# Block attention's pooled queries and output projection on four column groups of TensorE, in a new written order

## The chip, the cores and the metric

The kernel runs on one core of one Trainium2 chip. The metric is the device time of one launch, in microseconds (us). Three runs of the kernel before are shown, and one more execution was taken by the hardware profiler.

## The reference

A decoder of pre-norm layers over x of shape 8 x 256 x 256 (batch row, token, feature), all in fp32. The layers, each added to x, are:

- **a**: attention over features with 16 heads; **b**: a matrix-LSTM cell whose keys and values are the context; **c**: a product-key expert layer (64 gathers of 128 expert rows for each batch row) plus a gated MLP; **d**: causal single-head attention;
- **e**: block cross-attention, the layer that is changed here;
- then six layers of local attention with rotary embedding and a gated MLP.

Layer e, with x already normalised:

```
pooled = x.reshape(B, 16 blocks, 16, D).mean(axis=2)     # 16 pooled tokens of 256
q      = pooled @ Wq                                     # 16 x 1024 (16 heads of 64)
k, v   = ctx @ Wk, ctx @ Wv                              # 256 x 256 each, 4 kv heads
attn   = softmax(where(mask == 0, -1e9, q k^T / 8))
out    = (attn @ v).reshape(16, 1024) @ Wo               # 16 x 256
x     += each of the 16 rows of out, repeated 16 times
```

## The kernel before, in words

The kernel has two blocks, one after the other. `first_layers` computes layers a to e, `local_layers` the six local layers. A new block starts when every engine has ended the old one.

In `first_layers` each of the 8 batch rows passes through about eighty small pieces of work, named by layer (`a_q`, `c_up3`, `e_w0`). The order is written out by hand in `ORDER` (line 58), one list for each queue: tensor, scalar, vector, gpsimd, sync. An entry ("e_w0", -5) says that step s of the loop does this piece for batch row s - 5, so five or six batch rows are under way at once, and `pieces` (line 103) leaves out rows below 0 and above 7. Every engine works strictly through its own list; the lists meet at semaphores. `Slot` (line 240) deals seven PSUM banks out to the pieces of the tensor list in turn: a piece waits for the engine that copied out the piece seven places earlier in its bank.

Layer c sets the traffic between the engines. For each batch row POOL issues 16 groups `c_gather0` to `c_gather15` of four indirect DMAs (line 382) into a ring of four buffers (`RH = 4`). VectorE forms dot products of them (`c_dot`, line 1057), ScalarE a tanh (`c_tanh`) and diagonal matrices (`c_diag`, line 804), and TensorE adds the rows up (`c_up`, line 601), which gives the ring buffer back: `c_gather` j waits for `c_up` j - 4.

The pieces of layer e on TensorE are:

- `e_hT` turns the normalised tile; VectorE sums blocks of 16 tokens into `pooled`, 128 features x 2 halves x 16 blocks (line 1114).
- `e_w0`, `e_w1` (line 671) are the queries: `pooled` is the stationary operand, 128 rows by 16 columns, and 512 columns of `e_wq` stream past for each of two feature halves. Each fills partitions 0 to 15 of one PSUM bank. VectorE copies the first (line 863), ScalarE the second (line 757), into `e_flat`, 16 x 1024.
- `e_q` (line 681) turns that in eight transposes of 16 x 128, and ScalarE copies it to `e_qT`.
- `e_s0`, `e_s1` scores; softmax on VectorE and ScalarE; `e_pT` turns; `e_o` is probabilities times values.
- `e_y` (line 721) is the output projection: eight products, stationary 128 x 16 of `e_o`, moving 128 x 256 of `e_wo`, all added into partitions 0 to 15. ScalarE copies the 16 x 256 result.
- `e_u` (line 729) spreads each of the 16 rows over its 16 tokens with `unpool`, a 16 x 256 matrix of ones and zeros, and VectorE adds it to x.

A fp32 product is two passes through the array, so the trace has two matmuls for each `pe.matmul`; a transpose is one.

POOL makes the constants at the start (`start`, from line 337), and then takes up its list, which begins with `a_rstd` of row 0. SyncE loads the contexts: `b_ctx` (line 277) fills `ctx_b` and `ctx_one` and can begin when `b_cT`, `b_h0` and `b_h1` of the row before are done, and `b_cT`, a turn on TensorE (line 410), waits for it. In the tensor list `b_cT` of row s - 2 stands ten places behind `b_h1` of row s - 3.

Of the kernel before, what the change touches and what calls it, by code (L numbers as in the profile page):

```python
# [20 lines left out]
P = 128  # L21
BATCH, SEQ, D = 8, 256, 256
TILES = SEQ // P
KC = D // P
# [18 lines left out]
def first_layers(nc, xall, x_loaded, ident, ident_bf, shared, dram):  # L43
# [11 lines left out]
    SCALE = 1.0 / 8.0  # L55

# [9 lines left out]
        ("e_s1", -5), ("c_up7", -4), ("c_up8", -4), ("a_k", -1), ("c_up9", -4), ("e_v", -5), ("e_cT", -4), ("e_pT", -5), ("a_q", -1), ("e_o", -5),  # L66
        ("a_z", -1), ("e_y", -5), ("b_hT", -2), ("c_hT", -3), ("e_u", -5), ("c_q0", -3),
    ]
    ORDER["scalar"] = [
# [6 lines left out]
        ("c_diag8", -4), ("c_diag9", -4), ("b_cT", -2), ("e_exp", -5), ("e_v", -5), ("e_cT", -4), ("e_pT", -5), ("a_q", -1), ("e_o", -5),  # L76
        ("c_tanh10", -4), ("c_diag10", -4), ("e_y", -5),
    ]
    ORDER["vector"] = [
# [16 lines left out]
    ]  # L96
    ORDER["sync"] = [
        ("e_ctx", -5), ("e_mask", -4), ("b_ctx", -2),
    ]
    FIRST = max(ahead for order in ORDER.values() for _, ahead in order)  # L100
    LAST = -min(ahead for order in ORDER.values() for _, ahead in order)

# [1979 lines left out]
```

## Time and profile before

| | |
|---|---|
| median of 3 runs | 4052.93 us |
| lowest, highest | 4036.28, 4060.89 us |
| profiled execution | 4046.25 us |
| its span, first to last instruction | 4044.5 us |
| mean granted TensorE clock | 0.972 of full speed |
| first block (layers a to e) | 0 to 1085 us of the span |
| second block (six local layers) | 1085 to 4044.5 us |

Times in a row of the trace are from the start of the span. A line of a timeline gives start, duration, engine, source line, operation, tiles and shapes, the number of instructions merged into it and, in brackets, how long the engine idled before and for what. `128*16 128x256` is a product with a stationary operand of 128 rows by 16 columns and a result of 256 columns. The end of a matmul is modelled and includes the time in the pipeline, so what a piece takes of TensorE is read from the start of its first matmul to the start of the next piece.

### The profile page before, as it was taken

How to read it: one execution, taken by the hardware profiler on the slowest of the kernel's cores; microseconds unless marked ns; L12 is line 12 of the kernel's file. 1: busy time of each engine (PE TensorE's matmuls, PEld its weight loads, DVE VectorE, ACT ScalarE, POOL GpSimd, SP SyncE). 2: the span in 40 equal slices, each digit the busy share in tenths (PEclk: the TensorE clock that was granted, in tenths of full speed). 3: DMA queues.
4: the chain of work that ended last, by engine and by line, in shares of the span. 5: the costliest groups of instructions: out<-in, count | busy, mean ns of one | idle time of the engine just before them, and what ended most of it. 6: DMA issues, size and time to landing. Idle time of an engine off the chain costs nothing.

```text
span 4044.5 us, 75813 instructions
## 1 busy us (share of the span) xinstructions
PE 3814.3 (94%) x25720; PEld 2763.9 (68%) x25720; DVE 2827.7 (70%) x9152; ACT 2275.8 (56%) x6594; POOL 2242.3 (55%) x2091
## 2 busy tenths in 40 slices
PE   7699999897679999999999999999999999999998
PEld 5577777675346777777777777777777777777766
DVE  4577787775367777777777777777777777777763
ACT  2333443343256666666666666666666666666663
POOL 1555565566266555565565565556555556556540
PEclk8899999999789999999999999999999999999999
DMA  3655555567100001000100001000010000010000
GB/s 118 154 155 144 148 154 141 153 164 201 47 1 6 7 8 35 31 12 6 39 16 27 7 6 37 17 29 4 7 39 14 29 7 27 16 31 14 5 7 27
DMA packets 110543, 210.95 MB, mean 52 GB/s; under 512 B 22321, under 2 KB 71505, under 8 KB 108625
## 3 DMA queue, kind: packets, MB, share of 16 engines
q0 software_dynamic: 40960, 134.25, 12.7%
q1 hardware_dynamic: 69056, 71.71, 5.5%
q8 instruction: 210, 3.44, 0.4%
q14 instruction: 173, 1.41, 0.1%
q10 hardware_dynamic: 144, 0.13, 0.0%
HBM read 191.39 MB, written 2.10 MB: 48 GB/s over the span
## 4 chain that ended last, share of the span: by engine, by line
PE 67%; issue 2%; DVE 2%; POOL 1%; ACT 1%; DMA 0%; SPq 0%; DVEq 0%; POOLq 0%; ACTq 0%
PE pj L1594 23%; PE pj L1674 12%; PE y_ps L1657 8%; PE y_ps L1683 6%; PE sc L1622 5%; PE o_ps L1648 4%; PE tp L1633 4%; PE tp L1602 4%; PE tp L1572 1%; POOL l_qk_rot L1535 1%; ACT l_probs L1753 0%; DVE l_probs L1890 0%; POOL l_r_q L1540 0%; DVE l_qk_cos L1866 0%; POOL l_r_k L1540 0%
## 5 line engine op out<-in xcount | busy, mean ns | idle before, releaser
L1594 PE MATMUL pj<-w_qkv,l_xT 128*128 128x512 f32 x2304 | 1063.1, 598 | 7.2 <-DMA l_qk_gain<-in_gains 3.6
L1535 POOL TENSOR_TENSOR l_qk_rot<-l_qk_cos,l_qk_sin 128x512 f32<-128x512 f32 x384 | 564.8, 1471 | 840.5 <-DVE l_qk_sin L1869 555.7
L382 POOL DMA_INDIRECT f_rows<-in_emb,f_expert x512 | 514.6, 1005 | 382.2 <-PE facc L601 175.0
L1594 PEld LDWEIGHTS pj<-w_qkv,l_xT 128*128 128x128 f32 x2304 | 413.5, 191 | 385.8 <-issue 375.9
L1753 ACT ACTIVATE l_probs<-l_probs,l_low 128x128 f32<-128x128 f32 x1536 | 594.0, 391 | 2.4 <-DVE l_low L1890 0.6
L1674 PE MATMUL pj<-l_xnT,l_w 128*128 128x256 f32 x2112 | 510.9, 387 | 2.2 <-issue 1.2
L1861 DVE TENSOR_REDUCE l_ss<-l_qk_sq 128x8 f32<-128x512 f32 x384 | 261.6, 681 | 324.9 <-ACT l_qk_sq L1740 173.3
L1890 DVE CUSTOM_DVE_ANT_0 l_probs<-sc,l_shut,l_r_q 128x128 f32<-128x128 f32 x1536 | 440.2, 344 | 54.4 <-PE tp L1633 46.7
L1718 ACT ACTIVATE l_qk_raw<-pj 128x512 f32<-128x512 f32 x384 | 227.0, 591 | 434.6 <-PE pj L1594 419.6
L1674 PEld LDWEIGHTS pj<-l_xnT,l_w 128*128 128x128 f32 x2112 | 383.9, 190 | 65.0 <-issue 17.4
L1657 PE MATMUL y_ps<-w_o,l_oT 128*128 128x256 f32 x1536 | 341.2, 380 | 3.5 <-ACT l_oT L1718 3.5
L1657 PEld LDWEIGHTS y_ps<-w_o,l_oT 128*128 128x128 f32 x1536 | 292.8, 191 | 63.9 <-issue 22.0
L1540 POOL TENSOR_TENSOR l_r_q<-l_ssm,l_minus_half 128x8 f32<-128x8 f32 x192 | 320.4, 1669 | 16.0
L1540 POOL TENSOR_TENSOR l_r_k<-l_ssm,l_minus_half 128x8 f32<-128x8 f32 x192 | 320.4, 1669 | 16.0
L1866 DVE TENSOR_TENSOR l_qk_cos<-l_qk_raw,l_rope 128x512 f32<-128x512 f32 x384 | 302.2, 787 | 0.0
L601 PE MATMUL facc<-f_rows,f_diag 128*128 128x256 f32 x1024 | 266.5, 410 | 32.8 <-ACT f_diag L804 25.5
L1921 DVE TENSOR_SCALAR l_hT<-pj,l_ff_cols 128x256 f32<-128x256 f32 (+1 forms) x282 | 135.2, 480 | 231.6 <-ACT l_gate L1781 231.6
L1753 ACT ACTIVATION_READ_ACCUMULATOR l_probs<-l_probs,l_low 128x1 f32 x1536 | 291.8, 190 | 0.0
L1683 PE MATMUL y_ps<-l_w,l_hT 128*128 128x256 f32 x1128 | 266.3, 386 | 0.6 <-DVE l_hT L1928 0.6
L1633 PEld LDWEIGHTS tp<-identity,l_probs 128*128 128x128 f32 x1536 | 180.7, 141 | 119.4 <-issue 97.0
L601 PEld LDWEIGHTS facc<-f_rows,f_diag 128*128 128x128 f32 x1024 | 205.7, 207 | 78.7 <-issue 39.6
L1633 PE MATMUL tp<-identity,l_probs 128*128 128x128 f32 x1536 | 239.8, 279 | 14.6 <-DVE l_probs L1900 5.7
(324 smaller groups left out, 7164.6 us busy)
## 6 DMA issues: line engine op xcount, KB each, us to landing
w_qkv<-in_L_ffn_Wqkv SPq DMA_DIRECT2D x12, 1024.0 KB
l_w<-in_ff_w SPq DMA_DIRECT2D x6, 1408.0 KB, 6.1
f_rows<-in_emb,f_expert POOLq DMA_INDIRECT x512
w_o<-in_L_ffn_Wo SPq DMA_DIRECT2D x6, 1024.0 KB
w_qkv<-in_L_ffn_Wqkv SPq DMA_DIRECT2D x12, 512.0 KB
l_xf<-l_stream SPq DMA_DIRECT2D x48, 128.0 KB
l_xf<-l_stream SPq DMA_DIRECT2D x48, 127.0 KB
l_w<-in_ff_w SPq DMA_DIRECT2D x6, 768.0 KB, 4.9
```

The source lines that it names most:

```text
L382: pool.indirect_dma_start(rows[:, j % RH, k, :], None, dram["emb"], bass.IndirectOffsetOnAxis(ap=expert[:, n % 2, at:at + 1], axis=0)).the ...
L601: last = pe.matmul(acc[:, j // (HALVES // TILES), :], diag[:, j % 2, k, :], rows[:, j % RH, k, D:2 * D], start=(first and k == 0), stop=(f ...
L1535: pool.tensor_tensor(qk_rot[:, i % ROTS, :], qk_cos[:, b, :], qk_sin[:, b, :], ALU.add).then_inc(rotated if s == 0 else pool_front, 1)
L1540: pool.tensor_tensor(inv_norm, ssm[:, b, :], minus_half[:, :], ALU.pow).then_inc(pool_front, 1)
L1594: last = pe.matmul(pj[b][:, :], xT[:, k, t * P:(t + 1) * P], w_qkv[:, k, s * INNER + c * 512:s * INNER + (c + 1) * 512], start=(k == 0), s ...
L1633: last = pe.transpose(bank[:, at:at + P], probs[:, u % 2, 2 * p + x, t * P:(t + 1) * P], ident[:, :])
L1657: last = pe.matmul(y_ps[:, t, :], oT[:, k, t * P:(t + 1) * P], w_o[:, k, :], start=(t == 0 and k == 0), stop=(t == TILES - 1 and k == HP - 1))
L1674: last = pe.matmul(pj[b][:, s * SEQ:(s + 1) * SEQ], w_1[:, k, at:at + P], xnT[:, k, :], start=(k == 0), stop=(k == KC - 1))
L1683: last = pe.matmul(y_ps[:, t, :], hT[:, f, t * P:(t + 1) * P], w_2[:, f, :], start=(f == 0), stop=(f == FC - 1))
L1753: last = nc.scalar.activation(tile, tile, ACT.Exp, bias=low[:, u % 2, at, t:t + 1], scale=-1.0, accum_out=p_sum[:, u % 2, at, t:t + 1])
L1866: nc.vector.tensor_tensor(cos, raw, table(0, 0, DH), ALU.mult)
L1890: last = nc.vector.tensor_tensor_reduce(probs[:, u % 2, at, t * P:(t + 1) * P], sc[x][:, cols], shut[:, t, :], r_q[:, par, t, h:h + 1], 3. ...
```

## The change

It does four things.

1. `e_w0` and `e_w1` become one piece `e_w`. The 1024 query columns are taken as four groups of 256. Group g writes PSUM partitions 32g to 32g + 31, so each group uses its own 32 columns of the array. The stationary operand is 32 columns of `pooled`, 16 of them real and 16 that belong to the next half or to a new block of zeros. One copy (ScalarE, 128 x 256) takes the place of two, and `e_q` is two transposes of 128 x 128 in place of eight small ones, copied out by ScalarE with a strided view.
2. `e_y` is done the same way: four column groups each sum two of the eight products. The four partial sums stay on four sets of partitions, ScalarE copies 128 x 256, and `e_u` adds them, because `unpool` now has four copies of its pattern on 128 partitions, with zero rows between.
3. POOL makes two more zero fills and three copies of `unpool` (32 x 256 each) before its last constant semaphore.
4. All five lists of `ORDER` are new. `b_cT` moves to the start of the next step, behind `c_s2`; `b_ctx` comes first in SyncE's list; `f_rstd` stands before `c_gather14`; `c_y1` and many of the `c_m` and `c_up` pieces change places.

```diff
-        ("c_up5", -4), ("b_h0", -3), ("e_w0", -5), ("b_h1", -3), ("e_w1", -5), ("c_up6", -4), ("e_q", -5), ("a_hT", -1), ("b_cT", -2), ("e_s0", -5),
-        ("e_s1", -5), ("c_up7", -4), ("c_up8", -4), ("a_k", -1), ("c_up9", -4), ("e_v", -5), ("e_cT", -4), ("e_pT", -5), ("a_q", -1), ("e_o", -5),
-        ("a_z", -1), ("e_y", -5), ("b_hT", -2), ("c_hT", -3), ("e_u", -5), ("c_q0", -3),
+        ("c_q1", -4), ("c_q0", -4), ("e_cT", -5), ("b_hT", -3), ("c_s0", -4), ("c_s1", -4), ("c_up10", -5), ("c_s3", -4), ("c_s2", -4), ("b_cT", -3),
+        ("c_up11", -5), ("a_v", -2), ("c_m0", -4), ("c_m1", -4), ("c_m2", -4), ("c_m3", -4), ("c_m4", -4), ("c_up12", -5), ("b_g", -3), ("c_m5", -4),
...
+        ("b_qk2", -3), ("b_qk3", -3), ("e_hT", -5), ("c_up5", -4), ("b_h0", -3), ("b_h1", -3), ("a_hT", -1), ("e_w", -5), ("c_up6", -4), ("e_q", -5),
+        ("a_k", -1), ("e_s1", -5), ("e_s0", -5), ("c_up7", -4), ("a_q", -1), ("c_up8", -4), ("e_v", -5), ("c_y1", -4), ("e_pT", -5), ("c_up9", -4),
+        ("e_o", -5), ("a_z", -1), ("e_y", -5), ("c_hT", -3), ("e_u", -5),
...
-        ("c_gather13", -4), ("c_gather14", -4), ("a_rstd", 0), ("c_gather15", -4), ("f_rstd", -5), ("c_gather0", -3), ("c_gather1", -3),
+        ("f_rstd", -5), ("c_gather14", -4),
...
-        ("e_ctx", -5), ("e_mask", -4), ("b_ctx", -2),
+        ("b_ctx", -3), ("e_ctx", -4), ("e_mask", -4),
...
-        pooled = sb("pooled", [P, KC, NB])
+        pooled = sb("pooled", [P, KC + 1, NB])
...
+                pool.wait_ge(set_step, made[0])
+                for g in range(1, 4):
+                    pool.tensor_copy(unpool[g * QUAD:(g + 1) * QUAD, :], unpool[0:QUAD, :]).then_inc(set_step, 1)
...
-                    for k in range(KC):
-                        last = pe.matmul(s.bank[0:NB, :], pooled[:, k, :], e_wq[:, k, i * 512:(i + 1) * 512], start=(k == 0), stop=(k == KC - 1))
+                both = pooled[:, :, :].rearrange("p k n -> p (k n)")
+                for k in range(KC):
+                    for g in range(4):
+                        last = pe.matmul(s.bank[g * QUAD:(g + 1) * QUAD, 0:SEQ], both[:, k * NB:k * NB + QUAD], e_wq[:, k, g * 256:(g + 1) * 256],
+                                         start=(k == 0), stop=(k == KC - 1), skip_group_check=True)
...
-                for c in range(8):
-                    last = pe.transpose(s.bank[:, c * NB:(c + 1) * NB], e_flat[:, c * P:(c + 1) * P], ident[0:NB, 0:NB])
+                for c in range(2):
+                    last = pe.transpose(s.bank[:, c * P:(c + 1) * P], e_w[:, c * P:(c + 1) * P], ident[:, :])
...
-                for c in range(8):
-                    last = pe.matmul(s.bank[0:NB, 0:D], e_o[:, c * NB:(c + 1) * NB], e_wo[:, c, :], start=(c == 0), stop=(c == 7))
+                for h in range(2):
+                    for g in range(4):
+                        c = 2 * g + h
+                        last = pe.matmul(s.bank[g * QUAD:(g + 1) * QUAD, 0:D], e_o[:, c * NB:c * NB + QUAD], e_wo[:, c, :], start=(h == 0), stop=(h == 1), skip_group_check=True)
```

## Rows read from the trace of the kernel before

**Rows 1.** The page's head and its busy time of each engine.

```profile
span 4044.5 us, 75813 instructions
PE 3814.3 (94%) x25720; PEld 2763.9 (68%) x25720; DVE 2827.7 (70%) x9152; ACT 2275.8 (56%) x6594; POOL 2242.3 (55%) x2091
```

**Rows 2.** Busy time by stretch: bounds, length, PE, PEld, DVE, ACT, POOL, clock, DMA.

```profile
278.00:945.00 667.00, 614.53 (x3070) 475.64 (x3068) 507.29 (x2085) 258.78 (x787) 402.02 (x403) 0.96 0.58 152
945.00:1057.00 112.00, 72.80 (x298) 52.39 (x298) 43.52 (x184) 30.29 (x100) 49.94 (x50) 0.85 0.53 152
```

**Rows 3.** The block sums of line 1114, one for each batch row.

```profile
L1114 DVE TENSOR_REDUCE f_pooled<-fp x8: 691/691/692, 277.9 to 1056.7; 128x32 f32<-128x512 f32 x8
```

**Rows 4.** Waits of PE from 278 to 945 us: total, times, longest.

```profile
PE fp L410 <- DMA f_ctx_one<-in_ctx: 10.6, 5, 2.7
PE facc L601 <- ACT f_diag L804: 6.3, 4, 3.1
```

**Rows 5.** Timeline of PE around `e_w0`, `e_w1` and `e_q` of one batch row.

```profile
512.50 1.89 PE L601 MATMUL facc<-f_rows,f_diag 128*128 128x256 f32 x8
514.22 1.00 PE L535 MATMUL fp<-f_ctx_one,f_b_c 128*128 128x65 f32 x8
515.16 1.89 PE L671 MATMUL fp<-f_e_wq,f_pooled 128*16 128x512 f32 x4
516.98 0.44 PE L544 MATMUL fp<-f_ctx_one,f_b_c 128*128 128x65 f32 x2
...
518.91 1.89 PE L671 MATMUL fp<-f_e_wq,f_pooled 128*16 128x512 f32 x4
520.73 1.99 PE L601 MATMUL facc<-f_rows,f_diag 128*128 128x256 f32 x8
522.65 0.67 PE L681 MATMUL fp<-identity,f_e_p 16*128 16x16 f32 x8
523.25 0.66 PE L410 MATMUL fp<-identity,f_h_ad 128*128 128x128 f32 x4
```

**Rows 6.** Timeline of PE around `e_y` of the same batch row.

```profile
541.51 3.63 PE L721 MATMUL fp<-f_e_wo,f_e_o 128*16 128x256 f32 x16
545.07 0.66 PE L410 MATMUL fp<-identity,f_h_be 128*128 128x128 f32 x4
```

**Rows 7.** Timeline of PE in the second block: scores, then probabilities times values.

```profile
2006.49 1.10 PE L1622 MATMUL sc<-l_kT,l_qT 64*64 64x128 f32 x32
2007.53 3.72 PE L1674 MATMUL pj<-l_xnT,l_w 128*128 128x256 f32 x16
...
2012.92 0.44 PE L1648 MATMUL o_ps<-l_pT,l_v 128*64 128x128 f32 x4
2013.19 0.28 PE L1648 MATMUL o_ps<-l_pT,l_v_mid 128*64 128x64 f32 x4
...
2013.97 0.70 PE L1594 MATMUL pj<-w_qkv,l_xT 128*128 128x512 f32 x1
```

**Rows 8.** Timeline of PE at the end of the first block, batch row 7.

```profile
1057.50 5.13 PE L671 MATMUL fp<-f_e_wq,f_pooled 128*16 128x512 f32 x8 [0.83 <-issue]
1063.36 0.64 PE L681 MATMUL fp<-identity,f_e_p 16*128 16x16 f32 x8 [0.72 <-issue]
...
1077.05 5.62 PE L721 MATMUL fp<-f_e_wo,f_e_o 128*16 128x256 f32 x16 [0.37 <-ACT f_e_o L757]
1083.13 1.13 PE L729 MATMUL fp<-f_e_y,f_unpool 16*128 16x256 f32 x4 [0.46 <-ACT f_e_y L757]
```

**Rows 9.** POOL's gathers by line from 278 to 945 us: busy, mean ns, idle before.

```profile
L382 POOL DMA_INDIRECT f_rows<-in_emb,f_expert x367 | 369.4, 1007 | 262.1 <-PE facc L601 129.9 <-issue 104.1 <-remote 26.3
```

**Rows 10.** Timeline of POOL: a gather late in the first block.

```profile
1009.13 0.95 POOL L382 DMA_INDIRECT f_rows<-in_emb,f_expert  x1 [5.89 <-PE facc L601]
```

**Rows 11.** Timeline of POOL at the start of the span.

```profile
1.60 0.29 POOL L2002 CAST identity_bf<-identity 128x128 bf16<-128x128 f32 x1
...
9.55 0.72 POOL L369 TENSOR_TENSOR f_rstd_a<-f_var_eps_a,f_minus_half 128x2 f32<-128x2 f32 x1 [0.18 <-POOL f_g_raw L337]
```

**Rows 12.** VectorE's copy of `e_w0`: ns least, median, most.

```profile
L863 DVE COPY f_e_p<-fp x8: 678/679/679, 283.8 to 1061.0; 16x512 f32<-16x512 f32 x8
```

More of the change, by code:

```diff
@@ L662, in e_v_, with e_w_ @@
                 by_token("e_v", n, ctxT_e, e_wv)
-            def e_w(i):
-                def queries(n):
-                    pe.wait_ge(loaded["e"], 16 * LOADS["e"])
-                    pe.wait_ge(e_pooled, n + 1)
-                    s = Slot(f"e_w{i}", n)
-                    wait(pe, s.taken, s.before)
-                    for k in range(KC):
-                        last = pe.matmul(s.bank[0:NB, :], pooled[:, k, :], e_wq[:, k, i * 512:(i + 1) * 512], start=(k == 0), stop=(k == KC - 1))
-                    last.then_inc(ps_full, 1)
-                return queries
+            def e_w_(n):
+                pe.wait_ge(loaded["e"], 16 * LOADS["e"])
+                if n == 0:
+                    pe.wait_ge(consts_set, 2)
+                pe.wait_ge(e_pooled, n + 1)
+                s = Slot("e_w", n)
+                wait(pe, s.taken, s.before)
+                both = pooled[:, :, :].rearrange("p k n -> p (k n)")
[3 more added lines that the diff above has]
+                                         start=(k == 0), stop=(k == KC - 1), skip_group_check=True)
+                last.then_inc(ps_full, 1)
             def e_q(n):
-                copied("e_w0", n)
-                copied("e_w1", n)
+                copied("e_w", n)
                 s = Slot("e_q", n)
                 wait(pe, s.taken, s.before)
-                for c in range(8):
-                    last = pe.transpose(s.bank[:, c * NB:(c + 1) * NB], e_flat[:, c * P:(c + 1) * P], ident[0:NB, 0:NB])
+                for c in range(2):
+                    last = pe.transpose(s.bank[:, c * P:(c + 1) * P], e_w[:, c * P:(c + 1) * P], ident[:, :])
                 last.then_inc(ps_full, 1)
@@ L739, in _ @@
                        "b_h0": b_h0, "b_h1": b_h1, "c_q0": c_q(0), "c_q1": c_q(1), "c_y0": c_y(0), "c_y1": c_y(1),
-                       "d_q": d_q, "d_k": d_k, "d_v": d_v, "d_s": d_s, "d_pT": d_pT_, "d_o": d_o, "e_cT": e_cT, "e_k": e_k, "e_v": e_v_, "e_w0": e_w(0), "e_w1": e_w(1), "e_q": e_q,
+                       "d_q": d_q, "d_k": d_k, "d_v": d_v, "d_s": d_s, "d_pT": d_pT_, "d_o": d_o, "e_cT": e_cT, "e_k": e_k, "e_v": e_v_, "e_w": e_w_, "e_q": e_q,
                        "e_s0": e_s(0), "e_s1": e_s(1), "e_pT": e_pT_, "e_o": e_o_, "e_y": e_y_, "e_u": e_u})
@@ L830, in e_exp, with e_q @@
                 last.then_inc(e_exped, 1)
+            def e_q(n):
+                s = Slot("e_q", n)
+                act.wait_ge(ps_full, s.full)
+                wait(act, ps_full, last_before("e_q", n, "e_s0 e_s1"))
+                F(e_qT[:, :, :].rearrange("p a n -> p (a n)").rearrange("p (g c q) -> p g c q", g=4, c=2),
+                  s.bank[:, 0:2 * P].rearrange("p (c g q) -> p g c q", c=2, g=4)[:, :, :, 0:NB], ACT.Copy).then_inc(s.taken, 1)
             do = {f"b_m{h}": b_m(h) for h in range(H4)}
@@ L845, in _ @@
                 "e_cT": copy_of("e_cT", flat(ctxT_e[:, :, :]), "e_k e_v"), "e_k": copy_of("e_k", flat(e_kT[:, :, :]), "e_s0 e_s1"),
[L846 to L848 removed]
+                "e_v": copy_of("e_v", flat(e_v[:, :, :]), "e_o"), "e_w": copy_of("e_w", e_w, "e_pT", SEQ), "e_q": e_q, "e_exp": e_exp,
+                "e_pT": copy_of("e_pT", e_pT[:, :, :, :].rearrange("p t g n -> p (t g n)"), "d_o e_o"), "e_o": copy_of("e_o", e_o[:, 0:8 * NB], "e_y", 8 * NB),
+                "e_y": copy_of("e_y", e_y[:, :], "e_u", D)})
             for piece, n in pieces("scalar"):
@@ L1112, in e_hT @@
                 dve.wait_ge(ps_full, s.full)
-                wait(dve, ps_full, last_before("e_hT", n, "e_w0 e_w1"))
-                V.tensor_reduce(flat(pooled[:, :, :]), s.bank[:, :].rearrange("p (kb j) -> p kb j", j=BLK), AX, ALU.add).then_inc(e_pooled, 1)
+                wait(dve, ps_full, last_before("e_hT", n, "e_w"))
+                V.tensor_reduce(flat(pooled[:, 0:KC, :]), s.bank[:, :].rearrange("p (kb j) -> p kb j", j=BLK), AX, ALU.add).then_inc(e_pooled, 1)
                 dve.wait_ge(e_pooled, n + 1)
@@ L1178, in _ @@
                        "d_k": copy_of("d_k", flat(k_ad[:, :, :]), "a_z d_s"), "d_top": d_top_, "d_inv": d_inv_, "d_o": d_o,
[L1179 removed]
+                       "e_hT": e_hT, "e_mask": e_mask, "e_s": e_s, "e_low": e_low, "e_probs": e_probs, "e_u": add_tiles("e_u")})
             gained = False
```

38 lines of the change are left out of this document (18 added, 20 removed), and 37 rows, old and new, of the table ORDER.

## The prediction

> **What bounds the kernel now.** I read the page first, then busy time by stretch, then the waits of TensorE, and last its timeline around the changed pieces. The page alone shows PE busy for 94% of the span [rows 1], but that is a mean over two blocks, and the change touches only the first, which ends at 1085 us. The second block runs the same instructions afterwards, so I take its 2959 us as fixed.
>
> Inside the first block the block sums of layer e mark the beat: eight of them from 277.9 to 1056.7 us [rows 3], so (1056.7 - 277.9) / 7 = 111.3 us for a batch row. From 278 to 945 us, six such periods, PE is busy 614.5 of 667 us, VectorE 507, ScalarE 259, POOL 402 [rows 2]. POOL has a hidden part: between its gathers it idles for "issue" for 104 us in all [rows 9], which it cannot avoid, so it is occupied for 506 us. In order of occupation: PE 92%, VectorE 76%, POOL 76%. PE's own waits are small and scattered. The largest, 10.6 us in five waits, is the turn `b_cT` waiting for its context; the next is 6.3 us [rows 4]. A batch row therefore costs about 102.4 us of PE (614.5 / 6) and 8.8 us of idle. In these six periods a microsecond taken from PE is worth close to a microsecond. From 945 to 1057 us PE is busy only 72.8 of 112 us [rows 2]: the last row's gathers go round the ring with little beside them, and latency sets the time.
>
> **The price of a pass.** Eight passes of 256 columns take 514.22 - 512.50 = 1.72 us, 0.215 us each [rows 5]. So 128 columns cost about 0.108 us.
>
> **`e_w`.** Before, two pieces take 516.98 - 515.16 and 520.73 - 518.91, 1.82 us each, 3.64 us together [rows 5]. Afterwards it is 2 halves x 4 groups x 2 passes = 16 passes of 256 columns, the same number of streamed columns. All depends on whether the four groups stream side by side, which no row shows for four groups of 32 columns. The bounds: not at all side by side, 16 x 0.215 = 3.44 us, no gain; all four, 4 x 0.215 = 0.86 us. The nearest rows are two. The scores run in 64*64 tiles, two row halves and two column halves: 32 passes of 128 columns begin at 2006.49 and the next piece at 2007.53, 1.04 us against 32 x 0.108 = 3.46 us in series, 3.3 times faster [rows 7]. Probabilities times values use two column groups over all 128 rows: 8 passes of 128 and 16 of 64 columns would be 1.72 us in series and take 2013.97 - 2012.92 = 1.05 us, 1.6 times faster; their first four passes take 0.27 us where perfect pairs would need 0.22 [rows 7]. So different tiles overlap, four at once too, and products of two passes each do not prevent it. I take four at once, because the scores have four tiles in the same order of issue, and add 0.10 us for the irregular first pass: 0.96 us. The gain is 2.7 us.
>
> **`e_y`.** Before 545.07 - 541.51 = 3.56 us [rows 6]. After, 16 passes in four rounds as above, 0.96 us; gain 2.6 us.
>
> The Trainium skill ("TensorE: Matmul & The Clock Gate", the section on packing small matmuls) gives a speedup of 2.38 for three column groups and 3.07 for four row groups. With 3.07 in place of 3.6 each piece would take 1.12 us and the gain over eight rows would be about 2.6 us less; the 3.3 of rows 7 lies between. The skill's "TensorEngine Tiling", key properties, says that changing the tiling mode drains the engine, which speaks against two short tiled pieces between full-array ones; rows 5 to 7 show such a change at a tenth of a microsecond, and that is in my 0.96.
>
> **`e_q`.** Eight small transposes take 523.25 - 522.65 = 0.60 us [rows 5]. Two of 128 columns at 0.108 plus 0.10 are 0.32 us; gain 0.3 us. Bounds: 0.2 and 0.4.
>
> **`e_u`** keeps four passes of 256 columns; its contraction grows from 16 to 128 partitions. That could only matter if rows cost time; the 64-row and 128-row products of rows 7 are priced by columns. I take 0, bounds 0 and 0.2 us.
>
> **Sum for TensorE**: 2.7 + 2.6 + 0.3 = 5.6 us for a batch row.
>
> **Six full periods**: 6 x 5.6 = 33.6 us. The gaps that remain must not grow for this to hold.
>
> **The period 945 to 1057**: here a shorter `e_w` and `e_y` of row 6 help only where the ring waits for them. It does: POOL idled 5.89 us for a `c_up` that stands behind `e_y` and `e_u` [rows 10]. Bounds 0 and 5.6 us; I take 4.
>
> **The tail, row 7**: nothing stands beside layer e here, and the clock is often at its lower level. From the start of `e_w0` to `e_q` are 1063.36 - 1057.50 = 5.86 us; eight passes took 5.13 us, so four rounds of half the columns at that pace take 1.3 us, at the lower level 4 x 0.43 = 1.7 us, plus 0.4 us of pipeline and 0.5 us for one copy: 2.6 us, gain 3.2. `e_y` goes from 5.62 us [rows 8] to 1.0 to 1.9 us, gain 3.8. Together 7 us; bounds 5 and 8.
>
> **Order: `b_cT`.** It stands ten places behind `b_h1` of the row before, whose buffers its load needs, and waited 10.6 us in five rows [rows 4]. In the new order it stands in the next step, and the load is first in SyncE's list, so the transfer has more than 30 us of TensorE pieces over it. The waits vanish. But `b_hT` and `b_cT` leave the end of the step, where they covered `e_y`'s copy; `c_hT` (0.44 us) covers that now. What is late next is `c_up` behind `c_diag` (6.3 us, [rows 4]). I count half, 5 us; bounds 0 and 11.
>
> **Order, the rest**: `c_m0` to `c_m4` now stand in one run behind `a_v`, six pieces of 1.72 us, so `c_up11` and `c_up12` are 10.3 us apart, and `c_gather0` of the next row waits for `c_up12`. POOL has 27 us of waiting in a period ((129.9 + 26.3) / 6, [rows 9]) and must give up 5.6 of it. `f_rstd` before `c_gather14` costs nothing: it waits for the statistics behind `e_u`, and `c_gather14` waits for `c_up10`, which stands later than `e_u` on TensorE. I take 0; bounds a gain of 20 and a loss of 80 us (below).
>
> **Constants**: three copies of 32 x 256 and two fills on POOL stand before `a_rstd` of row 0, which starts right behind the constants at 9.55 us and on which the first turn waits. A cast of 128 x 128 took 0.29 us [rows 11]; three at 0.3 to 0.4, two fills and one more wait give 1.5 us of delay. Bounds 0.5 and 2.5.
>
> **Copies**: VectorE loses one of 0.68 us a row [rows 12], ScalarE's two become narrower in columns. Both engines are below 80%; what hides them is PE. I count 0.
>
> **Sum**: 33.6 + 4 + 7 + 5 - 1.5 = 48 us less than the profiled 4046.25 us, 3998 us. The median of the runs, 4052.9, lies 6.7 us above the profiled execution; from there it would be 4005. I forecast 4002 us.
>
> **Rivals.**
>
> *The period does not follow PE.* PE loses 5.6 us but the ring or VectorE's place in the order gives half back, or idler stretches bring more of the lower clock. The clock is 0.96 from 278 to 945 us [rows 2], so 8% of the time is at the lower level, costing at most 27 us; half as much again would take 13 us. For it: POOL's waits and the falls of the clock behind idle stretches. Against it: no engine but PE is above 80%. Saving 15 to 38 us, 4026 us.
>
> *Groups go two at a time.* Two full-height column groups are all that rows 7 show. Then `e_w` and `e_y` take 1.82 us each, 1.7 us a row more than forecast: 14 us, so 4016 us. *In series*: nothing is left but `e_q`, one copy and the order: 48 - 8 x 5.0 = 8 us, 4042 us; rows 7 speak against it.
>
> *The new order closes more gaps.* PE idles 8.8 us a period; were another 3 us of it gone, 6 x 3 = 18 us and some in the first 278 us: 3978 us.
>
> *Slower: the ring.* POOL's floor is 506 / 6 = 84 us a period, its waits 27. The run of `c_m` pieces between `c_up11` and `c_up12` makes `c_gather0` and all fifteen behind it late; TensorE then waits for `c_diag`. It decides once the waits pass 27 us a period. At 33 us, a period is 117 us: 7 x 6 = 42, less the tail's 7 and plus 1.5, 4083 us. Against it: before, `c_up10` and `c_up11` were nearly as far apart, about 9 us (three `c_m`, `e_k` and four `c_s`), and the ring bore it.
>
> **Chances.** Forecast 0.50 (3988 to 4014); more gaps closed 0.10; period follows by half 0.19; two at a time 0.07; in series 0.05; slower 0.09. A change below 1% (40 us) can't be told from none. Faster by over 1%: 0.8 of the forecast's 0.50, the 0.10, and 0.04 of the rest, 0.54. Slower by over 1%: 0.07. Within: 0.39. The range is 3976 to 4038: it leaves out the series case, the slower one and the end of the best one.
>
> **What would show it.** In the changed trace: `e_w` as 16 matmuls of `128*32 128x256` from whose first start to the next piece are about 1 us (2: two at a time; 3.5: series); the same for `e_y`; block sums 105 us apart; no wait of a turn for `f_ctx_one`; POOL's waits for line 601's successor below 20 us a period; the second block 2959 us long. I am wrong if the block sums stay 111 us apart while `e_w` takes 1 us: then PE was not what set the period.

## The result, and the profile after

The changed kernel took 4093.7 us, median of four runs (4082.0 to 4105.2), beside 4053.9 us of the kernel before in the same comparison: ratio 1.0104, 95% interval 1.0084 to 1.0125. It is 1% slower; the forecast was 4002 us. The profiled execution lasted 4082.0 us, its span 4080.3 us. The experiments below ran on several chips, and these split in two kinds: on three of them, the slow kind, the kernel before takes 4047 to 4055 us and the changed kernel loses about 1%; on two, the fast kind, the kernel before takes 3994 to 3995 us and the changed kernel gains 1.3%. The first comparison behaves as the slow kind. One slow chip was used in two comparisons and was slow in both; each of the others was used once, so that the kind belongs to the chip, and not to the hour, is likely and not shown. Most of what follows is the search for what the kinds differ in.

The page's head and the windows of the first comparison. Columns of the windows: stretch, its length, busy time of PE, PE's loads, VectorE, ScalarE, POOL, then granted clock, share of the DMA engines, GB/s.

```profile
span 4080.3 us, 75857 instructions
...
PE 3809.2 (93%) x25736; PEld 2777.8 (68%) x25736; DVE 2816.2 (69%) x9144; ACT 2272.3 (56%) x6594; POOL 2249.0 (55%) x2096
...
273.30:1015.80 742.50, 630.18 (x3156) 501.73 (x3155) 509.70 (x2132) 261.96 (x813) 426.24 (x423) 0.90 0.56 144
...
1097.00:1120.00 23.00, 15.07 (x78) 8.59 (x78) 6.51 (x9) 4.47 (x14) 0.00 (x0) 0.57 0.00 1
1120.00:4080.00 2960.00, 2897.47 (x21312) 2057.80 (x21312) 2107.41 (x6220) 1900.59 (x5465) 1673.26 (x1500) 0.99 0.06 18
```

The second block takes 2960 us, as before. The whole loss is in the first block, which ends at 1120 us in place of 1085. The rows are not of one length: the first six, from the first block sum to the seventh, take 695.0 us before and 742.5 us now, and the last one 83.8 and 81.0. So the comparison that counts is over those six rows, the first window above against the same one of the kernel before:

```profile
277.90:972.90 695.00, 632.61 (x3149) 490.50 (x3148) 518.26 (x2139) 266.26 (x813) 420.59 (x422) 0.96 0.58 153
```

The idle time of PE grew from 62 to 112 us. Its busy time is the same although each row gives it less to do, because the granted clock is 0.90 in place of 0.96: it falls behind the idle stretches, and the same matmuls then take longer. Idling and the lower clock together ate the saving. The marks of the beat, and the tiled matmuls (ns least, median, most; first and last start):

```profile
L682 PE MATMUL fp<-f_e_wq,f_pooled x128: 379/379/634, 277.3 to 1098.9; 128*32 128x256 f32 x128
L1133 DVE TENSOR_REDUCE f_pooled<-fp x8: 691/692/692, 273.3 to 1096.8; 128x32 f32<-128x512 f32 x8
```

The block sums are (1096.8 - 273.3) / 7 = 117.6 us apart, where [rows 3] had 111.3; this mean of seven is the "period" of the tables below. Now the waits of PE from 273 to 979 us (sum, times, longest), to be held against [rows 4]:

```profile
PE fp L691 <- ACT f_e_p L769: 18.9, 6, 3.8
PE fp L741 <- ACT f_e_y L769: 14.1, 2, 7.0
PE facc L598 <- DVE x_all L1108: 13.4, 2, 6.8
PE fp L741 <- issue: 10.9, 4, 6.3
```

`b_cT`'s wait for its context is gone, as forecast. In its place PE waits for ScalarE's copies of `e_w` and `e_y`, although a copy takes 0.38 us. The timelines of PE and of ScalarE over one batch row say why:

```profile
641.91 0.61 PE L418 MATMUL fp<-identity,f_h_ad 128*128 128x128 f32 x4
642.45 1.07 PE L682 MATMUL fp<-f_e_wq,f_pooled 128*32 128x256 f32 x16
643.45 1.30 PE L609 MATMUL facc<-f_rows,f_diag 128*128 128x256 f32 x4
...
648.96 0.44 PE L691 MATMUL fp<-identity,f_e_p 128*128 128x128 f32 x2 [1.75 <-ACT f_e_p L769]
```

```profile
641.37 1.26 ACT L816 ACTIVATE f_diag<-identity,f_coef 128x128 f32<-128x128 f32 x4
648.03 0.60 ACT L769 ACTIVATE f_hT_ad<-fp 128x512 f32<-128x512 f32 x1 [5.40 <-remote]
648.52 0.38 ACT L769 ACTIVATE f_e_p<-fp 128x256 f32<-128x256 f32 x1
```

The turn `a_hT` (the instructions of L418) ends at 642.5, `e_w` (L682) at 643.5 (1.0 us for 16 matmuls, as forecast), and the copies of both start at 648.0 and 648.5. ScalarE stood idle for 5.4 us, and VectorE, waiting for `b_h1`, as well. The releaser is given as "remote", which is what the view prints when a signal came and no instruction that gives it ended then. Elsewhere a waiting engine starts 0.04 to 0.07 us behind the end of the matmul. The ends of matmuls are modelled, but PE works in order and had long started the next piece. So by the trace the data were there, and the signal was not.

### The profile page after: what moved, and what is told of

Read it like the earlier page. It is cut to its first block, busy times and chain, and to the rows that moved or that the text cites. A ratio compares the mean times of both kernels' runs of the same rounds, so it can differ in the third digit from the quotient of the medians.

```text
span 4080.3 us, 75857 instructions
## 1 busy us (share of the span) xinstructions
PE 3809.2 (93%) x25736; PEld 2777.8 (68%) x25736; DVE 2816.2 (69%) x9144; ACT 2272.3 (56%) x6594; POOL 2249.0 (55%) x2096
## 4 chain that ended last, share of the span: by engine, by line
PE 66%; issue 2%; DVE 2%; POOL 1%; ACT 1%; DMA 0%; SPq 0%; DVEq 0%; POOLq 0%; ACTq 0%
PE pj L1613 23%; PE pj L1693 12%; PE y_ps L1676 8%; PE y_ps L1702 6%; PE sc L1641 5%; PE tp L1652 4%; PE o_ps L1667 4%; PE tp L1621 4%; PE tp L1591 1%; POOL l_qk_rot L1554 1%; ACT l_probs L1772 0%; DVE l_probs L1909 0%; DVE l_qk_cos L1885 0%; POOL l_r_q L1559 0%; DMA l_xf<-l_stream 0%
## 5 line engine op out<-in xcount | busy, mean ns | idle before, releaser
L609 PE MATMUL facc<-f_rows,f_diag 128*128 128x256 f32 x1024 | 279.4, 420 | 30.8 <-issue 15.5
```

The lines of the kernel that those rows point to most:

```text
L609: last = pe.matmul(acc[:, j // (HALVES // TILES), :], diag[:, j % 2, k, :], rows[:, j % RH, k, D:2 * D], start=(first and k == 0), stop=(f ...
```

## The experiments

In all tables "period" is the distance of the block sums, mean of seven. A signal is the increment of a semaphore, by which one engine tells another that it is done. "Silences" are pauses of over 2.5 us between two recorded signals of the compute engines (the DMA's signals left out) from 250 to 1130 us; they are counted from the signals' times in the trace, which the views don't print. Some belong to every kernel: on the fast kind there are 6 to 12 (22 to 41 us), most of them at the thinly filled end of the first block. On the slow kind a part of the signals is not recorded, so a pause can also be a lost record. A second measure is safer: "remote" is the sum of ScalarE's and VectorE's waits that have this releaser, as in the line at 648.03 us above, from 260 to 1130 us. A lost record can hide such a wait and can't make one. It is 0 in every kernel on the fast kind.

The expectations name theories by letters: T, the tiled pieces cost the time; O, the new order costs it; M, the late signals do; K, the kernel itself is slow at times; D, crowds of short matmuls bring the silences; P, TensorE's own work brings them; G, POOL's gathers bring them.

### First comparisons, which fell on the fast kind

`tiled_old_order`: the tiled pieces in the order of before (the list entries `e_w0`, `e_w1` become one `e_w`).

```diff
-("c_up5", -4), ("b_h0", -3), ("e_w0", -5), ("b_h1", -3), ("e_w1", -5), ("c_up6", -4), ("e_q", -5)
+("c_up5", -4), ("b_h0", -3), ("b_h1", -3), ("e_w", -5), ("c_up6", -4), ("e_q", -5)
```

> The tiled e_w, e_q, e_y and e_u in the order of the kernel before (e_w stands where e_w1 stood, e_w0's place is left out). Theory T, the tiled pieces themselves cost the time (they look 1 us long, but their copies start 5 to 7 us after their modelled end): block sums at least 116 us apart, first block about 1115 us, whole kernel 4080 to 4100 us. Theory O, the new order costs it: TensorE gets 5.6 us less a row and the period follows at least by half, block sums 105 to 109 us apart, 4005 to 4035 us.

`untiled_new_order`: the code of before with the new lists, `("e_w0", -5), ("e_w1", -5)` standing for `("e_w", -5)`.

> The new order with the pieces of the kernel before: e_w0 and e_w1 stand together where e_w stands, e_y is eight passes over 16 rows. Theory O (order): as slow as the changed kernel or slower, since TensorE has 5.6 us more to do a row, 4090 to 4140 us, block sums 117 to 123 us apart. Theory T (tiled pieces): the order is worth what its removed wait of b_cT is, so 4040 to 4060 us, block sums 110 to 112 us apart, and copies start at once when TensorE's pieces end.

`e_y_untiled` and `e_w_untiled`: the changed kernel with one of the two pieces put back.

```diff
-                for h in range(2):
-                    for g in range(4):
-                        ...
+                for c in range(8):
+                    last = pe.matmul(s.bank[0:NB, 0:D], e_o[:, c * NB:(c + 1) * NB], e_wo[:, c, :], start=(c == 0), stop=(c == 7))
```

> The changed kernel with e_y alone put back to eight passes into 16 rows (e_u takes 16 rows again). Theory T: half of the tiled pieces' cost goes, e_y's copy starts at the piece's end, 4065 to 4085 us. Theory O: e_y is 2.6 us longer in each row, so 4095 to 4115 us.

> The changed kernel with e_w alone put back to e_w0, e_w1 and the eight small transposes, e_y on four groups. Theory T, each four-group piece costs by itself: it lies between the new order without tiling (ratio 0.994) and with e_w tiled (0.990), or above both if e_y is the harmful one (0.995 to 1.005). Theory O, the order alone decides and a piece on four groups saves what its modelled time says, 2.6 us a row: 0.987 to 0.991.

`two_groups`: `QUAD = 64`, two column groups, `e_w[g * QUAD:(g + 1) * QUAD]` over 512 columns each, four transposes in `e_q`.

> The changed kernel with two column groups of 64 in place of four of 32: e_w is 8 passes of 512 columns in pairs, e_y 8 passes of 256 in pairs, e_q four transposes, partial sums in two groups. By the modelled times each piece takes 1.8 us in place of 1.0. Theory O: 1.6 us more a row, 4095 to 4115 us. Theory T, if the delay hangs on tiles of 32 columns: the delay goes, 4040 to 4065 us; if on tiling of any kind: 4090 to 4110 us and the same late copies.

The kernel before stood at 3995 us, so the changed kernel itself and the kernel before were run again:

> The changed kernel once more, since the four kernels run so far stood beside a kernel before of 3995 us, not 4053. If it loses 1% again (ratio 1.008 to 1.013), the copies that start 5 to 7 us after the modelled end of their pieces belong to the kernel and will be in this trace too. If the loss belongs to the chip of the first comparison, the late copies are gone (under 0.1 us) and the ratio is 0.985 to 0.995, as two groups and the e_y of before gave 0.987 and 0.990.

> The kernel before, for its trace under the same conditions as the others. Block sums 108 to 112 us apart; if PE's completion signals come in bunches only in the first comparison, every copy behind an idle ScalarE starts 0.04 us after its piece here.

| fast kind | us | ratio (95%) | period | silences |
|---|---|---|---|---|
| before_again | 3990.5 (before: 3993.9, 7 runs) | | 105.4 | 8, 31 us |
| tiled_old_order | 3992.6 | 0.9990 (0.9978 to 1.0002) | 106.5 | 12, 41 us |
| untiled_new_order | 3966.0 | 0.9938 (0.9918 to 0.9957) | 102.8 | 10, 36 us |
| e_y_untiled | 3954.1 | 0.9898 (0.9877 to 0.9918) | 101.0 | 6, 23 us |
| e_w_untiled | 3952.0 | 0.9897 (0.9880 to 0.9913) | 101.1 | 7, 26 us |
| two_groups | 3941.5 | 0.9869 (0.9852 to 0.9886) | 99.3 | 8, 27 us |
| changed_again | 3941.4 | 0.9869 (0.9853 to 0.9886) | 98.9 | 7, 22 us |

Theories T and O both fall on this kind: nothing costs time here, and the first four expectations all put the time too high. `before_again` has a period of 105.4 us where 108 to 112 were expected (its first six rows are 108.8 us each, the last one 85). The same program as in the first comparison gains 52 us. Its `e_y`, first PE, then ScalarE:

```profile
490.40 1.07 PE L733 MATMUL fp<-f_e_wo,f_e_o 128*32 128x256 f32 x16
491.40 0.65 PE L418 MATMUL fp<-identity,f_hc 128*128 128x128 f32 x4
491.98 1.13 PE L741 MATMUL fp<-f_e_y,f_unpool 128*128 128x256 f32 x4
```

```profile
491.54 0.38 ACT L769 ACTIVATE f_e_y<-fp 128x256 f32<-128x256 f32 x1 [0.68 <-PE fp L733]
```

The copy starts 0.07 us behind the piece, in each of eight rows. With the old order the tiles gain 0.1%, within the noise, and the waits of PE in `tiled_old_order` (267 to 920 us; the same two lines come out for 264 to 924) show where the gain went:

```profile
PE fp L418 <- DMA f_ctx_one<-in_ctx: 22.2, 5, 5.3
PE fp L418 <- DVE f_hc L914: 15.6, 6, 5.3
```

`before_again` waits 9.3 and 5.5 us there. Over the first six rows of each, PE's busy time fell from 618.6 to 593.6 us, 4.2 us a row, and `b_cT` and `c_hT` (the turns of L418 above), whose data come when they come, took 23 of the 25 us. For `b_cT` the list shows why: it is the fifth piece behind `b_h1`, not the tenth as the text ahead of the prediction has it, so four pieces cover the load of its context, and the tiles shorten two of them. The new order is what lets the tiles' gain through on this kind.

### Is it the chip, and what do late copies cost?

`changed_third` is the changed kernel again. `late_changed` and `late_before` hold back copies by hand (in `late_before` the piece `e_w1` stands for `a_hT`):

```diff
+                    for _ in range({"a_hT": 9, "e_y": 14}.get(name, 0)):
+                        chain.link(F(dst, s.bank[0:parts, 0:width], ACT.Copy))
                     F(dst, s.bank[0:parts, 0:width], ACT.Copy).then_inc(s.taken, 1)
...
+                    for _ in range(27 if t == 1 else 0):
+                        chain.link(V.tensor_copy(late[:, :], s.bank[:, 0:P]))
```

> The changed kernel once more, because two comparisons of it disagree: ratio 1.0104 with the kernel before at 4054 us, 0.987 with it at 3994 us. Theory M (the loss came with the silences of the engines' signals, which the first pair of traces shows and the later ones do not): if the kernel before takes about 3990 us here, the ratio is 0.985 to 0.989 and block sums are 101 to 105 us apart; if it takes 4040 us or more, the ratio is above 1.0 and silences of 3 to 7 us are back in the trace. Theory K (the kernel itself is sometimes slow): a ratio above 1.0 beside a kernel before of 3990 us.

> The changed kernel with three copies made late by hand in every row: VectorE does 27 small copies of a bank ahead of its work on b_h1, ScalarE repeats a_hT's copy nine times and e_y's fourteen times ahead of the one that signals, about 5.4 us each, at the places where the first trace of the changed kernel shows copies 5 to 7 us late. Theory M: the delays at b_h1 and a_hT lie beside each other, so the row is longer by most of 2 x 5.4 us, block sums 110 to 115 us apart in place of 102.3, 4000 to 4035 us. If ScalarE and VectorE have room for them (they are busy 40% and 75%), the row is longer by less than 4 us, 3940 to 3970 us, and theory M needs another path from the late signals to the period.

> The same delays in the kernel before: 27 small copies of VectorE ahead of its work on b_h1, nine more copies of e_w1, fourteen more of e_y, about 5.4 us each. If the order before bears late copies better than the new one (b_hT, b_cT and c_hT stand behind e_y, a wider cover), it loses 2 to 6 us a row, 4010 to 4040 us, and the changed kernel's gain is smaller or gone under delays. If both bear them alike, it loses what the changed kernel loses, 4050 to 4090 us, and the loss of the first comparison is due to where the silences fell, not to the order.

This chip was of the slow kind. `changed_third` took 4086.6 us beside 4048.3, ratio 1.0092 (1.0076 to 1.0109), with 47 silences, 194 us; the traces of the first comparison have 52 (204 us) for the changed kernel and 37 (131 us) for the one before, and on the fast kind the first five rows of these two kernels have none. This is theory M: the loss goes with the late signals. PE, ScalarE and POOL of `changed_third` around `e_y`:

```profile
560.77 1.07 PE L733 MATMUL fp<-f_e_wo,f_e_o 128*32 128x256 f32 x16
561.78 0.66 PE L418 MATMUL fp<-identity,f_hc 128*128 128x128 f32 x4
569.54 2.07 PE L741 MATMUL fp<-f_e_y,f_unpool 128*128 128x256 f32 x4 [7.11 <-ACT f_e_y L769]
```

```profile
560.57 1.26 ACT L816 ACTIVATE f_diag<-identity,f_coef 128x128 f32<-128x128 f32 x4
569.11 0.38 ACT L769 ACTIVATE f_e_y<-fp 128x256 f32<-128x256 f32 x1 [7.27 <-remote]
```

```profile
561.48 0.95 POOL L390 DMA_INDIRECT f_rows<-in_emb,f_expert  x1 [0.30 <-issue]
562.73 0.95 POOL L390 DMA_INDIRECT f_rows<-in_emb,f_expert  x1 [0.30 <-issue]
563.98 0.95 POOL L390 DMA_INDIRECT f_rows<-in_emb,f_expert  x1 [0.30 <-issue]
565.24 0.95 POOL L390 DMA_INDIRECT f_rows<-in_emb,f_expert  x1 [0.30 <-issue]
566.49 0.95 POOL L390 DMA_INDIRECT f_rows<-in_emb,f_expert  x1 [0.30 <-issue]
```

From row to row `e_y`'s copy starts 0.6, 6.4, 7.3, 6.6, 2.4, 2.3, 7.2 and 0.1 us behind its piece; in `changed_again` it is 0.07 us in all eight. The silence lies over a run of gathers 1.25 us apart. Two of its places come back in nearly every row (1 to 4 us and 32 to 37 us behind the block sum), in the first comparison and on this chip, but two thirds of the silences lie elsewhere. The delays by hand cost both kernels alike: `late_changed` took 4207.3 us (+121 against `changed_third`), `late_before` 4165.9 (+118 against 4048.3). I had expected 4000 to 4035 us and 4010 to 4040 or 4050 to 4090 us, with the fast kind in mind, and delays of 5.4 us each; what they tell is the difference, some 15 us a row. The delays were larger than meant on VectorE (18 of its copies take 5.8 us, so 27 take 8.7) and 5.6 and about 5.4 us on ScalarE. Late copies are dearly paid in either order, and the new order is not more tender; it meets more of them: ScalarE and VectorE wait 185 us for late signals in the changed kernel's first trace and 51 us in that of the kernel before.

### What brings the silences?

Theory D was that they follow crowds of short matmuls, of which the tiled pieces (16 in 1 us) make more.

```diff
-("c_up5", -4), ("b_h0", -3), ("b_h1", -3), ("a_hT", -1), ("e_w", -5), ("c_up6", -4), ("e_q", -5), ("a_k", -1)
+("b_h0", -3), ("c_up5", -4), ("b_h1", -3), ("a_hT", -1), ("c_up6", -4), ("e_w", -5), ("a_k", -1), ("e_q", -5)
```

That is `spread_changed`; `split_before` cuts the matmuls of before in quarters and halves. Its quarters share a bank, and of their partial sums only a part is kept, so it is read for its time alone:

```diff
+                        for q in range(4):
+                            last = pe.matmul(s.bank[0:NB, q * P:(q + 1) * P], pooled[:, k, :], e_wq[:, k, i * 512 + q * P:i * 512 + (q + 1) * P], ...
```

> The changed kernel with TensorE's list alone edited, so that long passes stand between the short ones: b_h0, c_up5, b_h1, a_hT, c_up6, e_w, a_k, e_q in place of c_up5, b_h0, b_h1, a_hT, e_w, c_up6, e_q, a_k, and a_z, e_pT, c_up9, e_o, c_y1, e_y in place of c_y1, e_pT, c_up9, e_o, a_z, e_y. Theory D: with the kernel before at 4050 us, the silences at +4 and +32 us shrink and the kernel is 20 to 80 us faster than the changed one, ratio 0.990 to 1.004; with the kernel before at 3990 us the edit does nothing, 0.985 to 0.990. If density is not the cause, it keeps the changed kernel's ratio on either chip, 1.009 or 0.987, within 0.003.

> The kernel before with the same columns in shorter matmuls: each matmul of e_w0 and e_w1 in four of 128 columns (16 a piece in place of 4), each of e_y in two of 128. By columns TensorE's time is unchanged. Theory D: with the kernel before at 4050 us it is slower by 15 to 80 us, ratio 1.004 to 1.02, with silences behind these pieces; with the kernel before at 3990 us there is no difference, 0.998 to 1.004. If density is not the cause, no difference on either.

> Two column groups of 64 again. Theory D (on some chips, those where the kernel before takes 4040 to 4060 us, dense runs of short matmuls bring silences of the signals; e_w and e_y on four groups are 16 matmuls in 1 us each, on two groups 8 in 1.8 us): with the kernel before at 4050 us here, ratio 0.990 to 1.003, so better than the changed kernel's 1.009, and the silences at +4 and +32 us of each row are shorter than 3 us. If only the chip and the order decide: ratio 1.007 to 1.015 there, same silences. With the kernel before at 3990 us: 0.987 again.

> The new order with the pieces of the kernel before again. With the kernel before at 4050 us here: theory D says the dense tiled pieces are gone, ratio 0.990 to 1.003, few silences; if the order itself is what meets the silences, ratio 1.010 to 1.020, as TensorE has 5.6 us more a row. With the kernel before at 3990 us: 0.994 again.

Theory D falls on every count: `split_before` is 1.0010, `spread_changed` at 1.0143 is slower than the changed kernel where the theory wanted it faster (and outside the 0.003 that "density is not the cause" allowed), and `untiled_new_2`, with no tiled piece in it, loses as much as the changed kernel. It is the order that loses on this kind, by 35 us, where it gains 29 on the other. The silences don't sort these kernels: `spread_changed` has 149 us of them and is the slowest, `split_before` has 155 and loses nothing. The waits for late signals do: 127 to 191 us in the four kernels with the new order, all of which lose, and 50 to 60 us in those with the old order, which don't. They still don't rank the four among themselves. Streaks of gathers, less than 1.7 us from start to start, were what was left. In the six rows behind the first block sum 39 of the 40 silences of `changed_third` begin inside a streak of four or more gathers, and such streaks cover 61% of that time. Streaks of eight or more are 12 to 16 in the old order (226 us in `before_again`) and 26 in the new one on the fast kind (412 us in `changed_again`); on the slow kind they are 16 (173 us) in the kernel before and about 30 (some 320 us) in `changed_third`. The new order keeps POOL's gathers running, which is what one wants of it. Two kernels test that: one leaves out three of four gathers, the other breaks the streaks and keeps all gathers.

```diff
-                    for k in range(HALF):
+                    for k in range(HALF if n == 0 else 1):
```

```diff
                         pool.indirect_dma_start(rows[:, j % RH, k, :], None, dram["emb"], ...)
+                    for _ in range(4):
+                        pool_chain.link(pool.tensor_copy(late[:, :], ident[:, :]))
```

> The changed kernel with fewer gathers: of the four gathers of each piece only the first is issued in the rows after the first one (the other slots keep old rows, so layer c adds something else); everything else is as it was. Theory G (on the slow kind of chip the signals fall silent where gathers follow each other without a pause; every silence seen stands in or behind such a streak): with the kernel before at 4050 us, no silences of over 2.5 us in rows 1 to 4, block sums 97 to 103 us apart, 3900 to 3960 us, as if on the fast kind. Theory P (the silences come from TensorE's own work, b_h1 and e_y above all): silences at +4 and +32 us stay, block sums 110 us or more apart, above 4000 us. With the kernel before at 3990 us both expect 3900 to 3945 us and nothing is told apart.

> The changed kernel with a pause on POOL behind each piece of four gathers: four copies of 128 by 128, about 1.4 us, 22 us a row, taken from POOL's slack. Theory G: with the kernel before at 4050 us the silences shrink and the ratio falls below the changed kernel's 1.009, to 0.990 to 1.004; with the kernel before at 3990 us POOL becomes nearly full and the row a little longer, 3945 to 3990 us. Theory P: with the kernel before at 4050 us the pauses only add, ratio 1.010 to 1.025.

Theory G held, with two misses in size. `fewer_gathers` on a slow chip:

```profile
273.00:779.00 506.00, 500.81 (x2719) 410.74 (x2719) 431.09 (x1800) 230.61 (x697) 112.08 (x113) 0.97 0.18 51
```

PE is busy 99% of five rows, and the first four are 101.8 us each, where those of `changed_again`, with all its gathers, are 102.7. No wait for a late signal is left, and four silences, none over 2.9 us (none were expected in rows 1 to 4; three are there). Leaving gathers out also takes work from POOL and from the DMA queues, and this kernel was not run on a fast chip; but the fast kind with all gathers is at 3941 us, so most of the 178 us between 4087 and 3908 us are what the slow kind had lost. With the pause silences fall from 194 to 55 us, the waits for late signals from 191 to 26 us and the ratio from 1.0092 to 1.0054, just above the 0.990 to 1.004 expected. The pause has its own price, since POOL is now nearly full: in six rows PE waits 54.6 us for normalised tiles (`h_ad`, `h_be`), which need a root that POOL takes. The last two runs halve the pause (two copies in place of four) and put the tiled pieces in the old order once more:

> The changed kernel with half the pause: two copies of 128 by 128 on POOL behind each piece of four gathers, about 0.7 us, 11 us a row. Theory G: with the kernel before at 4050 us, silences of over 2.5 us sum to between those of the changed kernel (194 us) and of the longer pause (55 us), and as POOL is less full the ratio is at or below the 1.005 of the longer pause, 0.995 to 1.006. With the kernel before at 3990 us the pause costs next to nothing, 0.987 to 0.992. If the gain of the longer pause was chance, it stays at 1.009 or more on the slow kind.

> The tiled pieces in the order of the kernel before again. With the kernel before at 4050 us: TensorE has 5.6 us less a row, but the streaks of gathers are those of the order before, so I expect as little as on the fast kind, ratio 0.995 to 1.003, and silences of about 130 us as in the kernel before; above 1.006 the tiled pieces would bring silences of their own. With the kernel before at 3990 us: 0.999 again.

| slow kind | us | ratio (95%) | period | silences | remote |
|---|---|---|---|---|---|
| changed_third | 4086.6 | 1.0092 (1.0076 to 1.0109) | 116.9 | 47, 194 us | 191 us |
| two_groups_2 | 4084.3 | 1.0099 (1.0078 to 1.0120) | 115.6 | 46, 172 us | 127 us |
| untiled_new_2 | 4085.7 | 1.0091 (1.0057 to 1.0126) | 114.9 | 45, 176 us | 136 us |
| spread_changed | 4104.1 | 1.0143 (1.0124 to 1.0162) | 118.5 | 38, 149 us | 130 us |
| split_before | 4056.1 | 1.0010 (0.9993 to 1.0027) | 113.5 | 42, 155 us | 60 us |
| tiled_old_2 | 4047.8 | 0.9989 (0.9974 to 1.0003) | 111.3 | 40, 144 us | 50 us |
| fewer_gathers | 3908.2 | 0.9652 (0.9621 to 0.9684) | 93.5 | 4, 11 us | 0 us |
| paced_gathers | 4069.9 | 1.0054 (1.0034 to 1.0073) | 115.3 | 17, 55 us | 26 us |
| paced_less | 4002.5 | 0.9880 (0.9852 to 0.9907) | 106.6 | 22, 73 us | 29 us |

`paced_less` beats both kernels on the slow kind: 1.2% faster than the kernel before, and 2.1% faster than the changed one by the two ratios (the two were run on different slow chips). I had expected 0.995 to 1.006; PE waits 31.3 us for those tiles here, not 54.6. Its POOL, by line (267 to 897 us: count, busy, mean ns, idle before) and as a timeline:

```profile
L394 POOL DMA_INDIRECT f_rows<-in_emb,f_expert x359 | 362.2, 1009 | 159.7 <-issue 110.6 <-DVE f_expert L1068 30.6 <-PE facc L615 11.9
L397 POOL COPY f_late<-identity 128x128 f32<-128x128 f32 x180 | 61.5, 342 | 6.1
```

```profile
498.88 0.95 POOL L394 DMA_INDIRECT f_rows<-in_emb,f_expert  x1 [0.30 <-issue]
500.13 0.95 POOL L394 DMA_INDIRECT f_rows<-in_emb,f_expert  x1 [0.30 <-issue]
501.08 0.83 POOL L397 COPY f_late<-identity 128x128 f32<-128x128 f32 x2
503.06 1.29 POOL L394 DMA_INDIRECT f_rows<-in_emb,f_expert  x1 [1.14 <-PE facc L615]
```

There are no more than four gathers in a row. The pause costs POOL 11 us a row of time that it spent waiting anyway: the gathers of `changed_third`, in its own line from 291 to 1027 us, waited 83.9 us for PE.

```profile
L390 POOL DMA_INDIRECT f_rows<-in_emb,f_expert x385 | 388.2, 1008 | 261.6 <-issue 112.6 <-PE facc L609 83.9 <-DVE f_expert L1062 48.4
```

## Why the prediction was wrong

**What bounds the kernel**: PE did, where signals come in time. On the fast kind PE is busy 580.4 of 613.7 us in six rows of the changed kernel, 95%. On the slow kind it is 627.2 of 736.3, 85%. Of these 123 us, 76 are more idling, and 47 are the same matmuls at a clock of 0.91 in place of 0.97. The prediction read the trace wrong in one place: 278 to 945 us are not six periods but 5.75, since six rows of the kernel before take 695 us; a row costs PE 105 us, not 102, and idles 10 us. And POOL's wait is (129.9 + 26.3) / 6 = 26 us, not 27. Neither slip changes the sum.

**`e_w`, `e_y`, `e_q`**: right. The first two run 1.0 us each, four groups at once, in the timelines of both kinds (0.96 forecast), `e_q`'s transposes take 0.27 us. On the fast kind PE's busy time fell by 5.7 us a row in the new order (`untiled_new_order` to `changed_again`, 614.8 to 580.4 us in six rows; 5.6 forecast) and by 4.2 in the old. What the row gained was less: in the new order 102.8 to 98.9, 3.9 us, and either piece alone gave half of that. On the slow kind it gained nothing. With two groups, whose two pieces take 1.87 and 1.88 us, 1.7 us more a row, the time is the same (3941.5 and 3941.4), so the last of the saving seems no longer to be on the path. This is the rival "period does not follow PE", in part, hidden behind the next term.

**Order: `b_cT`**: its wait vanished, as said. The order as a whole was worth far more than the 5 us I took: 29 us on the fast kind (ratio 0.9938); no run parts `b_cT` from the rest. Two errors of opposite sign made the sum right there, which was luck: the tiled pieces with their six periods, end and tail, less the constants, were put at 43 us and gave about 25, the order at 5 and gave 29; 48 us forecast, 52 measured.

**Order, the rest: "I take 0; bounds a gain of 20 and a loss of 80 us"**: this is the step that failed. On chips of the first comparison it costs 35 us and also swallows the tiles' gain, since `untiled_new_2` and `changed_third` have one ratio; the 33.6 us of the six full periods came to nothing, and the six rows took 47.5 us more. I had reasoned about which waits of POOL would grow and had not asked what a steadier stream of gathers does to the others. The sentence "the gaps that remain must not grow for this to hold" named the condition, and the late signals broke it: the gaps of PE grew from 62 to 112 us in the six rows, and the clock behind them fell from 0.96 to 0.90.

**The slower rival, the ring**, had 9% and 4083 us, close to what came, by another mechanism: POOL's waits for PE did not pass 27 us a row, they fell (129.9 us in [rows 9], 74.4 from 278 to 945 us now), and PE hardly waits for `c_diag` (2.6 us from 273 to 979 us). The number was luck.

**Tail and constants**: right in the main. From the last block sum to the end are 23 us, 28 before, so 5 us where 7 were forecast (bounds 5 and 8); the last row gave 2.8 us, forecast 4. The first `a_rstd` starts at 11.0 us in place of 9.55 [rows 11], 1.5 us later. The second block stayed 2960 us.

**Could it be seen before?** In part. The trace of before holds 37 silences. [Rows 9] had a third releaser, "remote 26.3", that I counted as waiting and did not look up. It is the mark of a signal that no instruction explains. ScalarE and VectorE had 51 us of it in that trace, none of which the rows show.

What stays open: what in the chip holds the signals back. A gather gives 16 signals, 1,024 a row. From row 1 to row 4 the fast kind's trace of the changed kernel holds 1,023 of them a row and 330 of the engines'; that of `changed_third` 514 and 240; that of `fewer_gathers`, on a slow chip, 254 of 256 and again 330. So lost records and late signals come and go with the gathers' signals together, as if both kinds of message shared a path that is narrower on some chips. That is argued, not shown. All traces and late starts come from recorded executions, and whether the recording itself holds the signals back was not tried. The rival that the slow kind's gathers or transfers are themselves slower is not borne out: both kinds run a gather in 1.01 us, and a packet of 4 KB takes 0.25 us on the slow kind and 0.26 to 0.27 on the fast. That `paced_less` keeps the 1.3% of the fast kind was not run: both paced kernels ran on slow chips.

## What to carry to other kernels

A gain on the busiest engine passes only as far as the waits behind it allow: on the fast kind the same tiled pieces gave 0.1% in one order and 0.7% in the other, on the slow kind nothing in either. Idle stretches cost twice: the time itself, and the lower clock of the matmuls behind them. An order that keeps a queue of indirect gathers full can cost more than it brings, as it did on the slow kind; look for copies that start microseconds behind the matmul they wait for, with "remote" as releaser, and try a pause of under a microsecond behind every few gathers. And where two comparisons disagree, look first at the kernel before: here its own time told the kind of chip.

## What the runs showed of the hardware

- Four column groups of 32 run side by side: 16 matmuls of 128x256 in 1.0 us (`after`; nearer the forecast 0.96 than the 1.12 it was set against), the four of a round 7 ns apart and a round every 0.216 us, the first 0.24 (`changed_again`). Two groups of 64 take 1.87 and 1.88 us for the same work (`two_groups`).
- In recorded executions on the slow kind, signals of the compute engines came up to 7 us late while gathers went on: `e_y`'s copy 7.27 us, with `e_y`'s own matmuls and the next piece long issued (`changed_third`). Signals held back arrive in a bunch: behind the ends of `b_h1`, `a_hT` and `e_w`, which lie 1.4 us apart, nothing is recorded until 647.95 us, and then signals at 647.95, 648.01, 648.15 and 648.17 (`after`).
- The same matmuls took 580 us of PE at a granted clock of 0.97 and 627 us at 0.91 (six rows, `changed_again` and `changed_third`).
- The time differs between chips: the same program took 3941 us on one and 4087 on another, and the kernel before 3994 and 4048, so the sign of a 1% change turned with it.
